# Mixing on halves of the array's rows, with a changed opening, in an f32 mixing and Strassen feed-forward kernel

## The reference

```
att   = softmax(mlp(cond))                     # 128 x 8, one row per batch
y[b]  = (sum_k att[b,k] * weight[k]) @ x[b] + att[b] @ bias_k      # 64 x 1024: the mixing
base  = y @ base_W.T                           # 8192 tokens, 1024 x 1024
w     = top-2 of softmax(y @ router_W.T), renormalised, dense over 8 experts
out   = x + base + 2 * sum_e (w_e * (y @ lora_A[e])) @ lora_B[e]
```

## Time and profile before

| | us |
|---|---|
| median of 3 runs | 962.93 (962.63 to 963.45) |
| the profiled execution, its own time | 962.68 |
| its span | 960.9 |
| PE busy | 951.2 |
| PEld busy | 878.3 |
| DVE busy | 743.2 |
| ACT busy | 236.9 |
| POOL busy | 294.4 |

### The profile page before, as it was taken

One profiled execution on the slowest core, in us unless ns is written; L12 is line 12 of the kernel. 1 busy time (PEld: TensorE's weight loads), 2 busy tenths in 40 slices (PEclk: granted clock), 3 DMA queues, 4 the chain that ended last, 5 costly groups with the idle time before them and its releaser, 6 DMA issues.

```text
span 960.9 us, 17804 instructions
## 1 busy us (share of the span) xinstructions
PE 951.2 (99%) x5765; PEld 878.3 (91%) x5765; DVE 743.2 (77%) x1641; ACT 236.9 (25%) x541; POOL 294.4 (31%) x228
## 2 busy tenths in 40 slices
PE   8999999999999999999999999999999999999997
PEld 6998999999999999999999999999999999999996
DVE  5877877877777877778777778777778777788774
ACT  5444212222222222222222122222122222222210
POOL 3002333133332133332233331333321333322331
PEclk9999999999999999999999999999999999999999
DMA  8666234333334332344242343332343323443311
GB/s 350 184 200 181 72 115 139 112 113 104 103 115 136 108 116 91 103 128 129 96 130 76 115 136 113 111 108 99 115 136 110 113 96 107 119 135 93 132 46 44
DMA packets 46694, 116.04 MB, mean 121 GB/s; under 512 B 20433, under 2 KB 20561, under 8 KB 45521
## 3 DMA queue, kind: packets, MB, share of 16 engines
q1 hardware_dynamic: 45824, 111.54, 35.2%
q0 software_dynamic: 576, 4.19, 2.1%
q10 hardware_dynamic: 272, 0.03, 0.0%
HBM read 77.97 MB, written 33.59 MB: 116 GB/s over the span
## 4 chain that ended last, share of the span: by engine, by line
PE 98%; DVE 1%; ACT 0%; issue 0%; POOL 0%; POOLq 0%; DVEq 0%; ACTq 0%
PE pc L499 17%; PE pa L510 13%; PE pb L510 13%; PE y_ps L471 12%; PE pb L513 9%; PE pa L513 9%; PE pd L499 9%; PE pd L554 4%; PE pc L554 4%; PE pc L536 1%; PE pd L536 1%; PE pa L524 1%; PE pb L524 1%; PE pd L544 1%; PE pa L527 1%; PE pb L527 1%
## 5 line engine op out<-in xcount | busy, mean ns | idle before, releaser
L471 PE MATMUL y_ps<-mix_w,x_sb 128*128 128x128 f32 x1024 | 193.9, 274 | 0.0
L394 POOL TENSOR_TENSOR out_sb<-out_sb,u 128x512 f32<-128x512 f32 x90 | 127.8, 1450 | 202.2 <-DVE u L1109 202.2
L471 PEld LDWEIGHTS y_ps<-mix_w,x_sb 128*128 128x128 f32 x1024 | 167.9, 190 | 12.3 <-issue 0.5
L364 POOL TENSOR_TENSOR ya<-ya 128x512 f32<-128x512 f32 x30 | 39.9, 1331 | 380.0 <-DVE ya L1014 380.0
L1014 DVE TENSOR_TENSOR ya<-y_ps,bias_sb 128x512 f32<-128x512 f32 x128 | 87.8, 687 | 37.5 <-PE y_ps L471 33.8
L499 PE MATMUL pc<-w_hi,s_hi 128*128 128x512 f32 x240 | 99.1, 413 | 0.0
L510 PE MATMUL pa<-w_hi,a_hi 128*128 128x376 f32 x240 | 94.6, 394 | 0.7 <-ACT p L825 0.7
L499 PE MATMUL pc<-w_hi,s_lo 128*128 128x512 f32 x240 | 94.4, 393 | 0.0
L499 PE MATMUL pc<-w_lo,s_hi 128*128 128x512 f32 x240 | 93.8, 391 | 0.0
L817 ACT ACTIVATE mid_hi<-pd 128x128 fp32r<-128x128 f32 x62 | 17.2, 278 | 273.2 <-PE pd L544 273.2
L810 ACT ACTIVATE exps<-logits,neg_max 128x8 f32<-128x8 f32 x64 | 19.3, 301 | 264.5 <-DVE neg_max L1031 264.5
(11 more groups left out here) (214 smaller groups left out, 2553.7 us busy)
## 6 DMA issues: line engine op xcount, KB each, us to landing
x_sb<-in_x SPq DMA_DIRECT2D x64, 512.0 KB, 3.8
out_sb<-in_x SPq DMA_DIRECT2D x64, 512.0 KB, 4.4
out<-out_sb SPq DMA_DIRECT2D x64, 512.0 KB, 2.8
w_raw<-in_base_t SPq DMA_DIRECT2D x5, 1024.0 KB, 11.3
w_raw<-neg POOLq DMA_DIRECT2D x4, 1024.0 KB, 10.4
bias_sb<-bias_rows SPq DMA_DIRECT2D x62, 64.0 KB, 4.8
w_raw<-in_side SPq DMA_DIRECT2D x1, 544.0 KB, 6.8
lb_raw<-in_lora_b SPq DMA_DIRECT2D x1, 512.0 KB, 14.1
```

What stands on the lines that cost most here:

```text
L364: nc.gpsimd.tensor_tensor(y_block(0, 1), y_block(0, 1), y_block(0, 0), ALU.subtract).then_inc(s3_set, 1)
L394: nc.gpsimd.tensor_tensor(o, o, u2[:, :], ALU.add).then_inc(done, 1)
L471: mm = nc.tensor.matmul(y_ps[q % 2][:, j * P:(j + 1) * P], x_sb[m][:, c * P:(c + 1) * P], mix_w[m][:, :], start=True, stop=True)
```

## The change

It rewrites the mixing: each batch is multiplied by itself, on the half of the array's rows on which it lies. `mix(n, h, k)` has 16 calls with 64 rows and 64 moving columns for every feature half, in the order m, j, b, with the two batches b of an m one after the other on the two row halves, each half with its own bank of `y_ps`. `mix_w[k][m]` is the plain sum (64 columns, two sets by the pair's parity), written by DVE itself; `place_mix`, its zeros and its semaphores are gone. The calls stand in two clusters: behind A11 and behind S3. A tile m now holds other batches, so x comes in two transfers of 256 KB per m, and the bias of a pair in one of 128 KB. `add_bias(n, h)` is two instructions, so four in a pair as before, and DVE's and ACT's orders follow (A11's split is earlier).

In the opening there are three products of zeros before the first table, other numbers and sizes of dummies, none between the bias's broadcast and the mixing; POOL does the spreading of the attention ahead of B11, whose low part it makes in four pieces; the first product does all its head columns, then waits for the low side columns, then does all its tails. The transfer of the bias rows to DRAM is issued by SP instead of ACT.

The diff, cut to its core:

```diff
...
-    x_t = x.rearrange("(t b) c d -> t (b c) d", b=PAR)
+    x_t = x.rearrange("(p b m) c d -> p m b c d", b=PAR, m=2)
...
-        mix_w = [place(f"mix_w{m}", P)[1] for m in range(2)]
-        bias_sb = [place(f"bias_sb{m}", P)[1] for m in range(2)]
+        mix_w = [[place(f"mix_w{k}{m}", C)[1] for m in range(2)] for k in range(2)]
+        _, bias_sb = place("bias_sb", 2 * PAR * C)
...
+            def read_x(n, m):
+
+                for b in range(PAR):
+                    sp.dma_start(x_sb[m][b * C:(b + 1) * C, :], x_t[n, m, b, :, :]).then_inc(x_in[m], 16)
...
+            def load_x(n):
+
+                sp.wait_ge(mixed, 2 * n)
+                for m in range(2):
+                    read_x(n, m)
+                sp.wait_ge(y_ready, 4 * n)
+                sp.dma_start(bias_sb[:, :].rearrange("p (s r) -> p s r", s=2),
+                             bias_dram.rearrange("s (p r) -> p s r", p=NP)[n, :, :].partition_broadcast(P)
+                             ).then_inc(bias_in, 16)
...
+            sp.wait_ge(bias_ready, 1)
+            sp.dma_start(bias_dram.rearrange("s (b c) -> b s c", b=B),
+                         bias_rows[:, :].rearrange("b (s c) -> b s c", s=2)).then_inc(bias_out, 16)
             sp.wait_ge(bias_out, 16)
-            for m in range(2):
-                load_x(1, m)
+            load_x(1)
...
-            for m in range(2):
-                load_x(2, m)
+            load_x(2)
             load_residual(1, 1)
 
             def body(p, k):
@@ -309,8 +312,7 @@
                 if not last(p):
                     load_residual(p + 1, 1 - k)
                 if mixes_after(p):
-                    for m in range(2):
-                        load_x(p + 2, m)
+                    load_x(p + 2)
 
             def store(p, k):
                 if plain(p):
@@ -343,16 +345,25 @@
 
             nc.gpsimd.affine_select(out=earlier, in_=earlier, compare_op=ALU.is_gt, fill=0.0,
                                     base=0, pattern=[[1, E], [-1, E]], channel_multiplier=0).then_inc(consts_set, 1)
-            for m in range(2):
-                nc.gpsimd.memset(mix_w[m][:, :], 0.0).then_inc(zeros_set, 1)
+            pool.wait_ge(pick_set, 6)
+            pool.wait_ge(att_step, 4)
+            nc.gpsimd.tensor_tensor(att_spread[:, :].rearrange("j (t k) -> j t k", k=K),
+                                    own_tile[:, :].unsqueeze(2).broadcast_to([P, NT, K]),
+                                    att_n[:, :].unsqueeze(1).broadcast_to([P, NT, K]), ALU.mult).then_inc(spread_set, 1)
 
             pool.wait_ge(a_in, 16)
             for n in range(WP):
                 nc.gpsimd.tensor_copy(w_hi[w_piece(B11, n)], w_raw[w_piece(T2, n)]).then_inc(w_hi_set[B11], 1)
-            for n in range(WP):
-                pool.wait_ge(w_hi_set[B11], n + 1)
-                nc.gpsimd.tensor_tensor(w_lo[w_piece(B11, n)], w_raw[w_piece(T2, n)],
-                                        w_hi[w_piece(B11, n)].bitcast(f32), ALU.subtract).then_inc(w_lo_set[B11], 1)
+
+            def quarter(blk, n):
+                at = blk * BLOCK + n * BANK
+                return slice(None), slice(at, at + BANK)
+
+            for n in range(HALF):
+                if n % (HALF // WP) == 0:
+                    pool.wait_ge(w_hi_set[B11], n // (HALF // WP) + 1)
+                nc.gpsimd.tensor_tensor(w_lo[quarter(B11, n)], w_raw[quarter(T2, n)],
+                                        w_hi[quarter(B11, n)].bitcast(f32), ALU.subtract).then_inc(w_lo_set[B11], 1)
...
-            def keep_warm(times):
-
-                for _ in range(times):
-                    nc.tensor.matmul(pb[:, 0:BANK], hot[:, 0:P], hot[:, :], start=True, stop=True)
-
+            def keep_warm(*columns):
+
+                for n in columns:
+                    nc.tensor.matmul(pb[:, 0:n], hot[:, 0:P], hot[:, 0:n], start=True, stop=True)
+
+            zeros = nc.const_aps.tensor(0.0, (P, P))
+            for _ in range(3):
+                nc.tensor.matmul(pb[:, 0:P], zeros, zeros, start=True, stop=True)
...
-            keep_warm(2)
+            keep_warm(512, 512)
             pe.wait_ge(params_in, 16)
             nc.tensor.matmul(mlp_ps[1][:, 0:P], w0_sb, cond_t, start=True, stop=True).then_inc(mlp_mm, 1)
-            keep_warm(1)
+            keep_warm(512)
             pe.wait_ge(mlp_act, 1)
             nc.tensor.matmul(mlp_ps[0][:, 0:P], w1_sb, h1[:, :], start=True, stop=True).then_inc(mlp_mm, 1)
-            keep_warm(1)
+            keep_warm(512, 256)
             pe.wait_ge(mlp_act, 2)
             nc.tensor.matmul(mlp_ps[1][:, 0:K], h2[:, :], w2_sb, start=True, stop=True).then_inc(mlp_mm, 1)
-            keep_warm(3)
+            keep_warm(512, 512, 512, 512)
             pe.wait_ge(att_step, 4)
             pe.wait_ge(pick_set, 2)
             for m in range(2):
                 nc.tensor.matmul(att_bc[:, m * K:(m + 1) * K], pick_half[:, m * P:(m + 1) * P], att_n[:, :],
                                  start=True, stop=True).then_inc(att_bc_mm, 1)
             nc.tensor.transpose(mlp_ps[0][0:K, 0:B], att_n[:, :], ident[:, :]).then_inc(att_tr, 1)
+            keep_warm(512)
             pe.wait_ge(bk_in, 16)
             pe.wait_ge(att_t_ready, 1)
             nc.tensor.matmul(bias_ps, att_t[:, :], bk_sb[:, :], start=True, stop=True).then_inc(bias_mm, 1)
-            keep_warm(1)
+            keep_warm(512, 256)
             pe.wait_ge(bias_ready, 1)
             for b in range(2 * PAR):
                 mm = nc.tensor.matmul(bias_bc[:, b * C:(b + 1) * C], pick_row[:, b * P:(b + 1) * P], bias_rows[:, :],
                                       start=True, stop=True)
             mm.then_inc(bias_bc_mm, 1)
-            keep_warm(2)
-
-            def mix_chunk(n, q, j):
-
-                m, h = q % 2, q // 2
-                if h == 0 and j == 0:
-                    pe.wait_ge(x_in[m], 16 * n + 16)
-                    pe.wait_ge(mix_set[m], PAR * n + PAR)
-                if j == 0 and not (first(n) and h == 0):
-
-                    pe.wait_ge(y_ready, 4 * n + q - 1)
-                c = h * HALF + j
-                mm = nc.tensor.matmul(y_ps[q % 2][:, j * P:(j + 1) * P], x_sb[m][:, c * P:(c + 1) * P],
-                                      mix_w[m][:, :], start=True, stop=True)
-                if j == HALF - 1:
-                    mm.then_inc(mixed, 1)
-
-            for q in range(4):
-                for j in range(HALF):
-                    mix_chunk(0, q, j)
-                if q == 1:
-                    pe.wait_ge(spread_set, 1)
-                    nc.tensor.matmul(pb[:, BANK:], parity[:, :], att_spread[:, :], start=True,
-                                     stop=True).then_inc(att_rows_mm, 1)
+
+            def mix(n, h, k):
+
+                if not (first(n) and h == 0):
+                    pe.wait_ge(y_ready, 4 * n + 2 * h)
+                for m in range(2):
+                    if h == 0:
+                        pe.wait_ge(x_in[m], 32 * n + 32)
+                        pe.wait_ge(summed_set, 2 * n + m + 1)
+                    for j in range(HALF):
+                        c = h * HALF + j
+                        for b in range(PAR):
+                            rows = slice(b * C, (b + 1) * C)
+                            to = y_ps[b][:, :].rearrange("p (s j m r) -> p s j m r", s=2, j=HALF, m=2)
+                            mm = nc.tensor.matmul(to[:, :, j, m, :], x_sb[m][rows, c * P:(c + 1) * P],
+                                                  mix_w[k][m][rows, :].rearrange("i (s r) -> i s r", s=2),
+                                                  start=True, stop=True)
+                mm.then_inc(mixed, 1)
+
+            mix(0, 0, 0)
+            pe.wait_ge(spread_set, 1)
+            nc.tensor.matmul(pb[:, BANK:], parity[:, :], att_spread[:, :], start=True, stop=True
+                             ).then_inc(att_rows_mm, 1)
+            mix(0, 1, 0)
...
                 if first(p):
+                    for j in range(HALF):
+                        pe.wait_ge(w_lo_set[B11], j + 1)
+                        for y, w, start, stop in plain_splits(*a11, j, True):
+                            plain_head(y, w, start, stop, B11, pa, j)
                     pe.wait_ge(side_lo_set, 1)
+                    for j in range(HALF):
+                        for y, w, start, stop in plain_splits(*a11, j, True):
+                            plain_tail(y, w, start, stop, B11, pa, j, 0)
                 else:
                     pe.wait_ge(plain_out, 1)
-                for j in range(HALF):
-                    wait_low(w_lo_set[B11], j)
-                    plain_with_side(*a11, B11, pa, j, 0, True)
+                    for j in range(HALF):
+                        plain_with_side(*a11, B11, pa, j, 0, True)
...
+                mm.then_inc(c21_mm, 1)
+                mix(p + 1, 0, 1 - p)
...
+                mix(p + 1, 1, 1 - p)
...
-                    mixed_in(0, j)
                     if j == 1 and not opening(p):
```

(63 more changed lines are left out.)

137 lines of the change are left out of this document (50 added, 87 removed).

## The result

The changed kernel takes a median of 989.38 us (988.78 to 991.14, 4 runs) against 963.05 us (962.63 to 963.45, 4 runs) before: ratio 1.0276, 95% interval 1.0259 to 1.0294. The profiled execution took 989.09 us, with a span of 987.3 us against 960.9. The forecast was 959.0 and faster; the time lies inside the range (945 to 1002) and on the other side of no change. Ratios compare fast executions alone, which leaves out one of run 7 (2436 us) and one of the kernel before (1040 us).

A forecast was written before the change was run, and what follows sets the result against it. TensorE's (PE's) own instruction stream was taken to bound the kernel. Mixing -1.9 us and opening -1.5 us sum to -3.4, from 962.9 to 959.5, say 959; range 945 to 1002, the forecast's own 955 to 966.

The forecast's parts named there:

- PE bounds the kernel, and time moves only if its stream does: Steady pairs: PE busy 29.13 of 29.13 us, so only a shorter or longer PE stream changes the time.
- rival (d): VectorE becomes late at u2 or A12 from bunched additions, 0.35 us a pair: about 970, down to no change; 8%.
- A load costs 0.107 to 0.111 whatever its height, and the loads of the halves overlap: Mixing: 64 half-height loads, side by side in the two halves, take 3.41 to 3.57 us per pair.
- (b): Mixing: loads of the two halves don't overlap, 7.1 us against 3.65 per pair, +111 us, about 1070; 11%.
- (c): Mixing: a half-height load is cheaper and matmul columns rule, -60 us, about 900; 9%.
- Switches: PE changes between full and half height four times a pair: taken as 0 each, bounds 0 to 0.35 us.
- the 0.06 that the forecast had right: Mixing on row halves: 3.59 us per pair against 3.65, -0.06 over 31 pairs, -1.9 us.
- rival (a): The height switches cost: 124 switches at 0.15 us are +19, at 0.35 +43; 975 to 1002, near 978; 21%.
- The opening, -1.5 us: Opening: first product near 19.1 us rather than 20.02, -0.9, with the clock -2.2; taken as -1.5.
- the forecast's far bound: Opening: the bounds around the -1.5 us taken were -3 and +1.5 us.
- SyncE's five transfers cost nothing: Steady pairs: SyncE issues five transfers for mixing instead of four per pair; x is still early enough, cost nothing.
- GpSimd's B11 comes 2 to 3 us later, still ahead of the product: Opening: spreading attention on GpSimd moves B11 from 13.8 to about 16.7 us, still ahead of the product.

The follow-up runs named there:

- run 7: Kernel before, with only the x transfers halved (two of 64 partitions per tile instead of one of 128): 966.26 us, ratio 1.0032.
- run 5: Changed kernel, with the calls of an m ordered by row half (four upper, then four lower) instead of alternating: 1030.08 us, ratio 1.0697.
- run 2: Changed kernel, with the same half-height calls in eight clusters of four per pair instead of two of sixteen: 1045.95 us, ratio 1.0869.
- run 3: Kernel before, with one extra full-height call (128 rows, 64 moving columns) per pair, its output overwritten: 968.87 us, ratio 1.0061.
- run 4: Kernel before, with one extra half-height call (64 rows, 64 moving columns) per pair, its output overwritten: 978.16 us, ratio 1.0162.
- run 6: Kernel before, with the changed opening's order alone (zeros, dummies, GpSimd spreading attention, low side last), mixing and x transfers as before: 959.93 us, ratio 0.9974.
- run 1: Kernel before, with its full-height mixing calls moved into two clusters per pair, behind A11 and behind S3: 961.27 us, ratio 0.9983.
- run 11: Kernel before, with the bias rows' transfer alone moved from ScalarE's queue to SyncE's: 963.07 us, ratio 1.0007.
- run 14: Kernel before, with the changed opening alone and the full-height clusters together, no half-height work: 959.71 us, ratio 0.9963.
- run 9: Changed kernel, with the opening's four half-height x transfers issued ahead of the first base block: 985.22 us, ratio 1.0237.
- run 12: Changed kernel, with the opening's lower x halves issued on ScalarE's queue, the upper by SyncE: 987.54 us, ratio 1.025.
- run 10: Changed kernel, with eight more 512-column dummies between the two tiles of the first mixing, in the wait for x: 990.78 us, ratio 1.0277.
- run 13: Changed kernel, with x ahead of the base block, bias rows on ScalarE, six full-height dummies before the first mixing cluster and two behind: median 986.06 us, ratio 1.0249.

## Why the forecast was wrong

- *PE bounds the kernel, and time moves only if its stream does*: right. VectorE and ScalarE never enter the steady pair's list; bunched additions cost nothing (VectorE 22.44 of 29.74 us), and rival (d) is out.
- *A load costs 0.107 to 0.111 whatever its height, and the loads of the halves overlap*: right. 16 slots of 0.111 per cluster. Rivals (b) and (c) are out with it; run 5 shows how near (b) was.
- *Switches: "I take 0, nearest to how every other load behaves"*: **this step failed**, and with it the sign. By the cluster's edges and by runs 2 to 4 a switch costs 0.17 us, so four per pair 0.67, less the 0.06 that the forecast had right: +0.61. In the 30 whole pairs that mix behind the first transpose this is 18.3, and small waits of early pairs (0.5 and 0.4) bring it to the 19.1 measured. The bounds (0 to 0.35) held it and rival (a) had it at 0.15, with +19 for the pairs. The fault was to price an operation that the trace doesn't show by the rows of operations of another kind: each load of the steady stream overlaps the matmul before it but none of them follows a matmul of another height. With only 0.06 us a pair to win, a tenth of the upper bound was enough to turn the sign; slower should have been the likelier side on these rows alone. The Trainium skill's "TensorEngine Tiling (Array Packing)", Key Properties, says that changing the tiling mode drains the engine; the trace agrees, with a load that starts only 0.07 us before the last matmul's modelled end at both edges, and 0.09 us in and 0.25 us out per cluster. It also says that different tiles load and multiply in parallel, and the 1.86 us for 32 loads agree.
- *The opening, -1.5 us*: wrong, +7.3. Its order of PE's work was a gain (run 6: -3.0 at the median, the forecast's far bound; the start of the mixing "near 12.8" should read 13.1 by its own terms, and was 13.02). **What failed here** is that the forecast counted SyncE's two more issues and took the transfers themselves as before. The whole rate is half (214 against 426 GB/s), by run 7 worth +3.9 us at the first product (23.93 against 20.02) with no other edit, and +3.2 at the median. The clock failed too: the forecast had only a possible gain for it. With full-height mixing and no wait for x it is full for good from a time between 14.4 and 17.4 us (before, runs 1, 3, 4, 6, 11, 14); with full height and the wait from 23.0 (run 7); with half height and no wait from 24.5 (run 9); with both, in the changed kernel and runs 2, 5 and 12, from a time between 25.6 and 31.8. How much the wait and how much the half-height calls hold it down is not separated.
- *SyncE's five transfers cost nothing* holds for the steady pair (29.13 in run 7). In the opening the bias rows' transfer moved past it, landing 18.1 us after issue instead of 8.2; alone it costs nothing (run 11), behind a repaired clock it is the next wait (run 10). I hadn't priced that move.
- *GpSimd's B11 comes 2 to 3 us later, still ahead of the product*: right in the change (16.9 instead of 13.8); in run 13 it is late, by the base block's transfer and not by the spreading.
- Of +26.4 us, then, 19.1 are rival (a) and 7.3 the opening, 5.2 of them at the first product (2.7 wait for x, about 4.0 slower work at 1.2 GHz, 1.6 given back) and 2.1 behind it (the clock, and 0.3 for the one cluster that lies ahead of the first transpose). The 19.1 come back in run 13 and rest on the runs; the split of the 7.3 is read from single executions, whose first product moves by over 4 us with the clock (run 2).

Open: why transfers to 64 partitions halve the rate of the whole, what holds the clock down, and the two later times of run 13.

## What to carry to other kernels

Before splitting a matmul over the array's row halves, price the weight loads: where they bound the stream, as with 128 columns loaded for 64 moving, the split saves nothing, and every return to full height costs. If half-height calls are needed, keep them in one stretch and alternate the halves call by call. Let transfers reach all 128 partitions, above all in an opening, where PE waits for them (3 us in run 7) and in the steady pairs it doesn't.

## What the runs showed of the hardware that was not expected

- A stay at half height costs 0.33 us whether it is one call (run 4), four (run 2) or 16 (0.34); full-height clusters cost nothing.
- Loads to the two row halves overlap fully when they alternate (0.111 us for two) and in part when eight loads of one half come first (2.47 against 1.86 us for 32).
- A transfer of 256 KB to 64 partitions took as long as one of 512 KB to 128 (4.3 against 3.8 us at the median), and while such ones ran in the opening (8 to 16 us, the changed kernel and runs 2, 5, 7, 10 and 12) the whole rate was 181 to 301 GB/s instead of 426, the DMA engines being as busy.
- With PE busy 8.00 of 8.00 us on half-height calls and what followed, its clock stood at 1.2 GHz (run 9, where it had fallen as the half-height calls began); in the one profiled execution with six full-height dummies ahead of them it stood at 2.4 GHz from 4.75 us on (run 13). Two of run 13's four executions took 8.5 us longer, so that the dummies are the reason isn't shown.
- The same opening had its first product at 20.78 and at 25.22 us in two executions, with the clock full from 5.1 to 15.3 in the first and only from 29.2 in the second (run 2 and the changed kernel).
